# A vision tower on one core: norms summed by accumulators, and a patch product split into float32r parts

## The reference, cut to what matters

```python
h = concat([cls, patches @ W_tok.T + b]) + pos           # 32 x 37 x 256
n = layernorm(h)                                         # then gamma, beta
z, c = sigmoid(n @ Wg.T + bg), n @ Wc.T + bc
hs = scan over tokens: s = (1 - z) * s + z * c           # along t
h = h + n + hs
g = gelu(layernorm(h) @ ternary(W_fc).T)                 # 1024 wide
h = h + (layernorm(g) * ln_w + ln_b) @ ternary(W_proj).T
h = h + attention(layernorm(h))                          # rope, causal, 37 x 37 per image
q = clip(round(layernorm(h) / scale), -127, 127)
h = h + (q * scale) @ (ternary_weight - 1).T + bias
# ternary(W) = sign(W) * min(round(|W| / gamma), 1), gamma = mean(|W|) + 1e-6
```

## Time and profile before

| | |
|---|---|
| median of 3 runs | 160.27 us (159.31 to 160.37) |
| the profiled execution | 159.69 us |
| its span in the trace | 157.9 us |
| mean granted TensorE clock | 0.978 |
| busy PE, DVE, ACT, POOL | 139.8, 126.4, 96.0, 87.2 us |

### The profile page before, as it was taken

One profiled execution on the slowest core, in us unless ns is written; L12 is line 12 of the kernel. 1 busy time (PEld: TensorE's weight loads), 2 busy tenths in 40 slices (PEclk: granted clock), 3 DMA queues, 4 the chain that ended last, 5 costly groups with the idle time before them and its releaser, 6 DMA issues.

```text
span 157.9 us, 3087 instructions
## 1 busy us (share of the span) xinstructions
PE 139.8 (89%) x874; PEld 111.3 (71%) x874; DVE 126.4 (80%) x404; ACT 96.0 (61%) x232; POOL 87.2 (55%) x159
## 2 busy tenths in 40 slices
PE   0599999999999996967996999789989989699993
PEld 0479898999889973545682757779878978596551
DVE  0031479989999998999996999699898979859893
ACT  3102288169264779999978785972476066368350
POOL 0000183455353657288995539989845786663530
PEclk9999999999999999999999999999999999869995
DMA  5999996000410000096595755797310000000243
GB/s 163 258 398 425 421 391 238 2 0 0 124 46 0 2 2 2 18 119 133 125 111 104 162 113 108 147 106 149 60 55 0 4 0 0 2 4 0 65 144 103
DMA packets 25621, 17.00 MB, mean 108 GB/s; under 512 B 20069, under 2 KB 23173, under 8 KB 25349
## 3 DMA queue, kind: packets, MB, share of 16 engines
q1 hardware_dynamic: 25605, 16.81, 40.3%
HBM read 9.70 MB, written 1.21 MB: 69 GB/s over the span
## 4 chain that ended last, share of the span: by engine, by line
DVE 26%; PE 22%; POOL 21%; issue 11%; ACT 8%; DMA 6%; SPq 4%; DVEq 0%; POOLq 0%; ACTq 0%
POOL small L1540 8%; DMA w_out_int<-w_out_in 6%; PE bank L661 5%; SPq L463 4%; POOL keys L1619 4%; POOL small L1535 4%; PE bank L758 3%; DVE stats L1093 3%; DVE gw L1414 3%; DVE gl L1106 2%; PE bank L832 2%; PE bank L792 2%; DVE rope L1460 2%; POOL small L1544 2%; POOL residual L1592 2%
## 5 line engine op out<-in xcount | busy, mean ns | idle before, releaser
L1540 POOL TENSOR_TENSOR small<-small,powers 128x1 f32<-128x1 f32 (+4 forms) x48 | 39.7, 826 | 6.0 <-DVE small L1403 2.8
L661 PE MATMUL bank<-w_tok,x_raw 128*128 128x256 f32 x108 | 27.7, 411 | 5.8 <-DMA w_tok<-w_tok_in 5.6
L661 PEld LDWEIGHTS bank<-w_tok,x_raw 128*128 128x128 f32 x108 | 21.5, 206 | 8.8 <-issue 5.6
L1535 POOL TENSOR_SCALAR small<-small 128x1 f32<-128x1 f32 x36 | 9.4, 260 | 24.9 <-DVE small L1101 23.2
L537 PE MATMUL bank<-pj,gt_hi 128*128 128x256 f16 x72 | 16.2, 273 | 0.7 <-issue 0.7
L537 PE MATMUL bank<-pj,gt_lo 128*128 128x256 f16 x72 | 16.2, 273 | 0.0
L932 ACT ACTIVATE n<-residual,small 128x256 f32<-128x256 f32 x18 | 10.7, 595 | 9.0 <-POOL small L1544 9.0
L537 PE MATMUL bank<-fc,n1t_hi 128*128 128x512 f16 x36 | 13.6, 379 | 0.6 <-ACT g L1002 0.3
L537 PE MATMUL bank<-fc,n1t_lo 128*128 128x512 f16 x36 | 13.6, 379 | 0.0
L1460 DVE SCALAR_TENSOR_TENSOR rope<-bank,packed,consts 128x324 f32<-128x324 f32 (+2 forms) x24 | 13.1, 608 | 0.3 <-POOL query L1613 0.2
L932 ACT ACTIVATE s<-end,small 108x256 f32<-108x256 f32 (+2 forms) x12 | 7.2, 596 | 9.4 <-POOL small L1544 6.2
(11 more groups left out here) (199 smaller groups left out, 411.7 us busy)
## 6 DMA issues: line engine op xcount, KB each, us to landing
x_raw<-x_in SPq DMA_DIRECT2D x9, 384.0 KB, 7.8
out_dram<-end SPq DMA_DIRECT2D x10, 108.0 KB
w_fc<-w_fc_in SPq DMA_DIRECT2D x1, 1024.0 KB, 10.0
w_pj<-w_pj_in SPq DMA_DIRECT2D x1, 1024.0 KB, 13.0
w_tok<-w_tok_in SPq DMA_DIRECT2D x2, 384.0 KB, 4.6
w_gate<-w_gate_in SPq DMA_DIRECT2D x1, 512.0 KB, 7.3
w_qk<-w_qk_in SPq DMA_DIRECT2D x1, 512.0 KB, 12.5
ln_w<-ln_w_in SPq DMA_DIRECT2D x1, 512.0 KB, 3.6
```

The costliest lines, as they stand in the source:

```text
L661: mm(out[:, 0:D], x_raw[:, i, k, :], w_tok[:, k, :], start=(k == 0), stop=False)
L1535: return nc.gpsimd.tensor_scalar(small[0:n, i, out:out + 1], small[0:n, i, value:value + 1], factor, add, ALU.mult, ALU.add)
L1540: return gt(small[0:n, i, r:r + width], small[0:n, i, ve:ve + width], powers[0:n, 0:width], ALU.pow)
```

## The change

**Patches.** Tiles 0 and 1 stay as they are (`PLAIN = 2`). For tiles 2 to 8, ACT copies the tile (128x768) into x_hi, rounded to float32r, and the DVE writes the rest x_lo over x_raw. w_tok is split once in the same way (128x1536 on either engine). `tok` then takes 18 float32r products instead of 6 float32 ones. x_hi has three slots, which lie over the memory of the scan's result, so that `scan:0` waits for the last `tok`, and `split:5` and later wait for the `tok` three tiles before.

**Norms 1 to 3.** BN_STATS and BN_AGGR go. The DVE instruction that makes the new residual (h1, proj, attend, c_row) leaves its row sum in an accumulator. ACT squares the centred tile with an accumulator (step `sq`) in place of the Identity, a small DVE instruction makes the mean, and POOL applies mean and scale by one tensor_scalar over 128x256 (L1619 of the changed kernel) in place of the shift. For norm 0 the statistics stay on the DVE, and the application goes from the DVE to POOL.

**Weights.** The ternary weights come from ACT: scale and round in place (`w_round`), then Sign (`w_sign`), both 128x2048 for each weight. The DVE's four instructions go.

**Narrow products.** The norm bias is made of 16 products of 2 columns (`w_ln_col`), a DVE sum and two float32 products of 128 columns that spread it. The class sums 0, 1 and 3 take one product each, from an accumulator.

```diff
@@ -33,6 +33,8 @@
...
+PLAIN = 2
+X_SLOTS = 3
@@ -125,59 +127,60 @@
...
-        c_h0:0 w_ones:0 w_pos:0 c_mean:0 c_var:0 w_small:0 stats0:0 mean0:0 stats0:1 stats0:2 c_norm:0 mean0:1
...
+        w_ones:0 w_pos:0 w_tok:0 stats0:0 mean0:0 split:2 w_gate:0 c_h0:0 split:3 stats0:1 c_mean:0 split:4 mean0:1
@@ -345,6 +355,8 @@
...
+    x_hi = m.at("x_hi", [X_SLOTS, KX, TILE], F32R, b_at + both)
+    assert X_SLOTS * KX * TILE * 4 <= both
@@ -573,15 +587,25 @@
...
                 pe.wait_ge(s["ln_b_hi_ready"], 1)
                 pe.wait_ge(s["ln_b_lo_ready"], 1)
-                split_product(out[:, 0:D], [
-                    (part[:, k:k + 1].to_broadcast([128, 128]), pj[:, k, :])
-                    for k in range(KH) for part in (ln_b_hi, ln_b_lo)
-                ]).then_inc(s["pe_ln_bias"], 1)
+                for b in range(KD):
+                    last = split_product(out[:, 2 * b:2 * b + 2], [
+                        (pj[:, k, b * 128:(b + 1) * 128], ln_b_both[:, k, :]) for k in range(KH)])
...
+            def w_ln_bias(_i):
+                out = claim(NARROW, ("ln_bias", 0))
...
+                for k in range(KD):
+                    last = mm(out[:, k * 128:(k + 1) * 128],
+                              derived[:, D_LN_COL + k:D_LN_COL + k + 1].to_broadcast([128, 128]), ident,
+                              start=True, stop=True)
@@ -590,11 +614,11 @@
...
-                    columns = range(C_SOURCE[n], C_SOURCE[n] + KD)
-                split_product(out[:, 0:1], [(ones[:, :], cls[:, c:c + 1]) for c in columns])\
+                    column = C_HSUM + n
+                mm(out[:, 0:1], ones[:, :], cls[:, column:column + 1], start=True, stop=True)\
@@ -654,11 +678,23 @@
...
-                    mm(out[:, 0:D], x_raw[:, i, k, :], w_tok[:, k, :], start=(k == 0), stop=False)
+                if i < PLAIN:
+                    pe.wait_ge(dma_x[i], 16)
+                    for k in range(KX):
+                        if i == 0 and k % (KX // 2) == 0:
+                            pe.wait_ge(s["dma_w_tok_b" if k else "dma_w_tok"], 16)
+                        mm(out[:, 0:D], x_raw[:, i, k, :], w_tok[:, k, :], start=(k == 0), stop=False)
+                else:
+                    if i == PLAIN:
+                        pe.wait_ge(s["wt_hi_ready"], 1)
+                        pe.wait_ge(s["wt_lo_ready"], 1)
+                    pe.wait_ge(s["x_hi_ready"], i - PLAIN + 1)
+                    pe.wait_ge(s["x_lo_ready"], i - PLAIN + 1)
+                    for k in range(KX):
+                        hi, lo = x_hi[:, i % X_SLOTS, k, :], x_lo[:, i, k, :]
+                        mm(out[:, 0:D], hi, wt_hi[:, k, :], start=(k == 0), stop=False)
+                        mm(out[:, 0:D], hi, wt_lo[:, k, :], start=False, stop=False)
+                        mm(out[:, 0:D], lo, wt_hi[:, k, :], start=False, stop=False)
@@ -890,6 +926,21 @@
...
+            def w_round(n):
+                _, w, _ = ternary[n]
+                act.wait_ge(s["cut_ready"], 2)
+                act.wait_ge(s["round_ready"], 2)
+                go(w[:, :, :], w[:, :, :], ACT.Identity, scale=derived[:, D_INV_GAMMA + n:D_INV_GAMMA + n + 1],
+                   bias=derived[:, D_ROUND:D_ROUND + 1]).then_inc(s["rounded_ready"], 1)
+            def w_sign(n):
+                out, w, ready = ternary[n]
+                act.wait_ge(s["rounded_ready"], n + 1)
+                go(out[:, :, :], w[:, :, :], ACT.Sign, bias=derived[:, D_ROUND + 1:D_ROUND + 2]).then_inc(s[ready], 1)
@@ -920,6 +971,17 @@
...
+            def w_tok_(_i):
+                act.wait_ge(s["dma_w_tok"], 16)
+                act.wait_ge(s["dma_w_tok_b"], 16)
+                go(wt_hi[:, :, :], w_tok[:, :, :], ACT.Copy).then_inc(s["wt_hi_ready"], 1)
+            def split(i):
+                act.wait_ge(dma_x[i], 16)
+                if i - PLAIN >= X_SLOTS:
+                    act.wait_ge(s["pe_tok"], i - X_SLOTS + 1)
+                go(x_hi[:, i % X_SLOTS, :, :], x_raw[:, i, :, :], ACT.Copy).then_inc(s["x_hi_ready"], 1)
@@ -937,29 +999,24 @@
...
+            def squares_of(norm):
+                def stage(i):
+                    h, ready, total, slot, free = summed[norm]
+                    n = end_rows(i) if norm == 3 else 128
+                    act.wait_ge(s[ready], i + 1)
+                    if i >= 2:
+                        act.wait_ge(s[free], i - 1)
+                    if i == 0 and norm == 2:
+                        act.wait_ge(s["pe_fold"], KD)
+                    if i == 0 and norm == 3:
+                        act.wait_ge(s["pe_gate"], 4 * CHUNKS)
+                    go(slot[0:n, i % 2, :], h[0:n, i, :], ACT.Square, bias=small[0:n, i, total:total + 1], scale=-float(D),
+                       accum_out=small[0:n, i, total + 1:total + 2]).then_inc(s[f"mv{norm}_ready"], 1)
+                return stage
@@ -1102,11 +1159,30 @@
...
+            def mean_of_sum(norm):
+                def stage(i):
+                    n = norm_rows(norm, i)
+                    dve.wait_ge(s[normed[norm][1]], i + 1)
+                    ts(col(i, MEANS[norm], 1, n), col(i, normed[norm][2], 1, n), 1.0 / D, None, ALU.mult)\
+                        .then_inc(s[f"mean{norm}_ready"], 1)
+                return stage
...
             def w_ones(_i):
                 nc.vector.memset(ones[:, :], 1.0).then_inc(s["ones_ready"], 1)
+                nc.vector.memset(derived[:, D_ROUND:D_ROUND + 1], ROUND).then_inc(s["round_ready"], 1)
+                nc.vector.memset(derived[:, D_ROUND + 1:D_ROUND + 2], -ROUND).then_inc(s["round_ready"], 1)
+            def w_tok_(_i):
+                dve.wait_ge(s["wt_hi_ready"], 1)
+                low_part(wt_lo[:, :, :], w_tok[:, :, :], wt_hi[:, :, :].bitcast(F32), s["wt_lo_ready"])
+            def split(i):
+                dve.wait_ge(s["x_hi_ready"], i - PLAIN + 1)
+                low_part(x_lo[:, i, :, :], x_raw[:, i, :, :], x_hi[:, i % X_SLOTS, :, :].bitcast(F32), s["x_lo_ready"])
@@ -1196,23 +1272,17 @@
...
-            def w_below(n):
-                out, w, _ = ternary[n]
-                dve.wait_ge(s["cut_ready"], 2)
-                ts(out[:, :, :], w[:, :, :], derived[:, D_NEG_CUT + n:D_NEG_CUT + n + 1], None, ALU.is_lt)\
-                    .then_inc(s["below_ready"], 1)
-            def w_ternary(n):
-                out, w, ready = ternary[n]
-                dve.wait_ge(s["below_ready"], n + 1)
-                stt(out=out[:, :, :], in0=w[:, :, :], scalar=derived[:, D_CUT + n:D_CUT + n + 1], in1=out[:, :, :],
-                    op0=ALU.is_gt, op1=ALU.subtract).then_inc(s[ready], 1)
+                ts(derived[:, D_GAMMA:D_GAMMA + 2], total, 1.0 / (HID * D), ABS_EPS, ALU.mult, ALU.add)\
+                    .then_inc(s["cut_ready"], 1)
@@ -1332,12 +1405,8 @@
...
             def n0_(i):
                 dve.wait_ge(s["r0_ready"], i + 1)
-                if i >= 2:
-                    dve.wait_ge(s["pe_t0"], i - 1)
                 shift(i, NB0, MV0, R0, "nb0_ready")
                 ts(col(i, NB0 + 1), col(i, R0), 1.0, None, ALU.add).then_inc(s["nb0_ready"], 1)
-                ts(n0[:, i % 2, :], h0[:, i, :], col(i, MV0), col(i, R0 + 1), ALU.subtract, ALU.mult)\
-                    .then_inc(s["n0_ready"], 1)
@@ -1376,6 +1445,8 @@
...
+                if n == 0:
+                    dve.wait_ge(s["pe_tok"], TILES)
                 if c > 0:
                     dve.wait_ge(s["hs_ready"], n - 1)
@@ -1385,7 +1456,8 @@
             def h1_(i):
                 dve.wait_ge(s["pe_hs"], i + 1)
                 dve.wait_ge(s["res0_ready"], i + 1)
-                tt(res[:, i, :], narrow(("hs", i)), res[:, i, :], ALU.add).then_inc(s["h1_ready"], 1)
+                stt(out=res[:, i, :], in0=narrow(("hs", i)), scalar=1.0, in1=res[:, i, :], op0=ALU.mult, op1=ALU.add,
+                    accum_out=col(i, MV1)).then_inc(s["h1_ready"], 1)
@@ -1539,10 +1614,10 @@
...
+            def applied(out, h, i, mv, r, n=128):
+                return nc.gpsimd.tensor_scalar(out, h[0:n, i, :], small[0:n, i, mv:mv + 1], small[0:n, i, r:r + 1],
+                                               ALU.subtract, ALU.mult)
@@ -1573,13 +1648,24 @@
...
+            def n0_(i):
+                pool.wait_ge(s["r0_ready"], i + 1)
+                if i >= 2:
+                    pool.wait_ge(s["pe_t0"], i - 1)
+                applied(n0[:, i % 2, :], h0, i, MV0, R0 + 1).then_inc(s["n0_ready"], 1)
             def h1_(i):
                 pool.wait_ge(s["mv1_ready"], i + 1)
-                scaled(i, VE1, MV1 + 1, 1.0, LN_EPS).then_inc(s["ve1_ready"], 1)
+                scaled(i, VE1, MV1 + 1, 1.0 / SQUARED, LN_EPS).then_inc(s["ve1_ready"], 1)
                 pool.wait_ge(s["ve1_ready"], i + 1)
                 power(i, VE1, R1).then_inc(s["r1_ready"], 1)
+            def n1_(i):
                 pool.wait_ge(s["r1_ready"], i + 1)
-                shift(i, NB1, MV1, R1, "nb1_ready")
+                if i >= 2:
+                    pool.wait_ge(s["pe_t1"], i - 1)
```

(2 more changed lines are left out.)

263 lines of the change are left out of this document (137 added, 126 removed).

## The result

The changed kernel takes **169.25 us**, median of four runs (167.54 to 171.16), against 160.32 of the kernel before in the same session: ratio 1.051, 95% interval 1.042 to 1.060. Two of the four runs are near 171 (the profiled one among them, 171.16 with a span of 169.4) and two near 167.6, and every ratio in this document is taken over the quicker runs of both kernels, while medians are over all runs. The forecast was 156.0. The sign is wrong, and the time lies outside the range.

The account below looks back on a forecast made before the run. No engine bounds the whole: PE decides from 20 to 60 us, the DVE leads the MLP, POOL beside it at its end. Front -1.7, MLP -0.8 and attention -1.2 from 159.69 gave 156.0 us, range 151.0 to 162.3.

Parts of the forecast that it names:

- Norms in the MLP: 60 to 110 us: DVE relief of 2.35 us against 1.6 for POOL's applications at 0.6 each; -0.8 us.
- The attention's term: 110 to 150 us: PE gains half of its 2.5 us idle time as the DVE loses 3.8; -1.2 us.
- The rival on POOL: MLP's end and attention: applications stretched to 1.1 us make POOL the bound; 162.3 us, chance 0.19.
- The hole at the start: PE before tile 2: waits for class token's sum, tile 2 at 15.9 to 17.0; 1.2 us lost.
- Patches: Tiles 2 to 8 on PE: 18 products in 2.08 us instead of 2.41; 2.3 us saved over seven tiles.
- Splits: Front: each tile costs the DVE 0.92 and ACT 0.8 us, w_tok some 1.8 and 1.5; nothing beyond the start.
- Front: Up to the first gelu: mean of PE's -2.1 us and ACT's -1.2; -1.7 us.
- Norm bias and class sums: Weight stages on PE: narrow products save 0.9 us on the norm bias and 0.1 on each class sum.
- ACT in the front: 20 to 60 us: ACT's busy time rises from 26.98 to 37.8 of 40 us.
- The rival, that no engine reaches such a share without loss: Front: ACT becomes the bound, its work taking 42 us at 90% busy; 159.9 us, chance 0.17.
- Norm rows on the DVE: MLP: 0.32 us less for each of some 15 norm rows, 4.8 us of DVE, of which 2.35 count.
- The rival that the MLP follows the DVE: 60 to 110 us: the DVE leads everywhere, so all 4.8 us count; 152.0 us, chance 0.22.

Follow-up runs that it names:

- e1: The kernel before with 14 extra POOL instructions of several forms in its idle time at the start; 158.75 us in one run.
- e3: The changed kernel with the class token's sum moved back to first place in the DVE's row; 167.05 us, ratio 1.047 to the kernel before.
- e5: e3 with the 39 POOL applications as a product of two tensors, the mean not subtracted; 154.41 us, ratio 0.964 to the kernel before.
- e15: e8 with the DVE's sum placed early and the spreading product and its DVE step moved behind the second h1; 161.66 us, ratio 1.011.
- e4: The changed kernel with all 39 norm applications on the DVE, the other engines' orders kept; 192.53 us, ratio 1.206 to the kernel before.
- e6: The kernel before with split patches and the ternary weights on ACT, norms as before, orders by hand; 171.48 us, ratio 1.061.
- e7: e6 with the narrow norm bias as well, orders by hand; 171.55 us, ratio 1.063 to the kernel before.
- e13: e4's instructions (applications on the DVE) in orders from a second, more robust search; 158.51 us, ratio 0.987 to the kernel before.
- e14: e7's instructions (norms as before) in orders from a second, more robust search; 155.76 us, ratio 0.978 to the kernel before.
- e8: The kernel before with the narrow norm bias alone; 162.61 us, ratio 1.008.

## Why the prediction was wrong, by its steps

**The step that failed** is, in "Norms in the MLP": "It has one, so I take 0.6, +0.22 each", with 0.38 to 0.728 as bounds and 1.1 as the end with stretch. The application takes 1.22 bare (e1) and 1.47 on the mean in norms 1 and 2, so the change is +1.09 each and not +0.22. The end of 1.1 was meant for applications stretched beside the DVE, and the price is above it without any. The reasoning behind it was that an instruction with one full input cannot cost more than one with two. e1 shows the reverse on POOL: 1.22 and 0.93 with one input and two or one operands by column, 0.61 with two inputs. The other bound, a shift of one column (0.378), says nothing of the 256 elements: e1 has 0.39 at the least for one column in the application's form and 1.22 for 256. I had no row of a wide tensor_scalar on POOL, and should have set a bound above the sum's 0.728, not only for stretch.

By the forecast's own formula 1.47 gives the MLP 15 x 1.09 x half - 2.35 = +5.8 in place of -0.8. Measured in e3: +2.2 (54.9 to 57.1), so less of the price showed there than the formula's half. The attention's term, -1.2, became +6.4 with the tail (43.3 to 49.7), which the forecast had at nothing: on POOL 12 applications of norm 3 take 14.8 us there in e3, where before 13 small shifts took 3.4. A part of the 6.4 is the clock, 0.90 on the mean there in e3 and 0.92 before. With the price taken back (e5) the same stages read -1.2 and -0.7 against before; the forecast had -0.8 and -1.2, and the front gave -4.0 for -1.7. So behind the front the sum held within 0.5 us a stage once its largest term had the price that it assumed (0.71 in e5, 0.6 in the forecast); that e5's 154.4 lies below 156.0 is the front's doing.

**The rival on POOL** had the mechanism and the place right, the end of the MLP (15.59 of 16.6 busy) and the attention, and its sign, applications above 1 us, came. The point from which it decides, about 1.0, no run tests: there are 0.71 (faster) and 1.4 (slower). It was given 0.19 and priced at 1.1, 162.3, which made the range end there. At the bare 1.22 it would already have passed. The rule that I quoted from the Trainium skill (GPSIMD Engine Reference, "Key points"), that elementwise work runs about twice as fast on VectorE, deserved more weight: by it and the 0.403 of the earlier trace rows an application would take some 0.8, an estimate, and that is above my bound of 0.728. The trace goes beyond it: 1.22 bare on POOL against 0.403 for the same tensor_scalar on the DVE, three times.

**The hole at the start**: forecast 15.9 to 17.0, near 16.4; measured 16.40, so the hole against 15.55 is 0.85, where the sum took 1.2. The wait that I named is there: the class token's sum is done on the DVE at 15.59, within the 15.1 to 16 of the forecast. Beside it stands one that I had not named: ACT's copy of tile 1 out of its bank, behind a split and the gate's high part, is done at 15.67, and it is the releaser that the trace gives. In e3, with `c_h0:0` in front, only that copy is left, and tile 2 starts at 15.59, near its place before; the class token's sum was worth 0.8. No term had the granted clock of 0.50 behind the hole in the profiled execution, some 3 us. Before, small products of PE filled the 0.87 us ahead of tile 2 almost wholly, and the clock was 1.00 there; after, PE had a pause of 1.68.

**Patches**: 18 products in 2.09 us (26.92 to 29.01), forecast 2.08. **Splits**: DVE 0.955 and 1.76, forecast 0.92 and 1.8; ACT 0.836, forecast 0.8. **Front**: forecast -1.7 with the hole in it; the first gelu of the changed kernel's trace is at 62.02, +2.3. With the hole repaired it is -1.5 (e3), close to the forecast by luck: without the 1.2 of the hole the forecast's way of reckoning gives some -2.3 (PE -3.3, ACT -1.2, for which it shows no working). With the POOL price gone as well it is -4.0 (e5). So the applications ahead of the first gelu, nine of norm 0, which I had called hidden in POOL's idle half, and two of norm 1, held it up by 2.5. That is a second term put at nothing.

**Norm bias and class sums**: the products cost what was forecast (0.55 for 0.54), but the term of 0.9 was not on the path. A stretch without idle time of PE is no proof that each microsecond taken from PE shortens it; with the DVE at 93% PE only waited instead (e15: 2.31 us of new waits, both for the DVE).

**ACT in the front**: 37.8 of 40 forecast, 37.61 in e3 and 39.60 in e5. The rival, that no engine reaches such a share without loss, is refuted by e5.

**Norm rows on the DVE**: 0.144 and an accumulator read of 0.083 for 0.413 and 0.171, so -0.357 each, forecast -0.32. The DVE was right to be unburdened, and it had the gain: 43.68 of 50 for 46.18, 2.5 us less, where the forecast had some 4. It went unused while POOL was late (e3), and part of it showed once POOL was not (e5).

**The rival that the MLP follows the DVE** can't be judged as a whole; e5, with POOL out of the way, gains 1.2 there and not 4.8, so the full count was too much.

## What to carry to other kernels

Where a change puts wide work on an engine that has only done narrow or different work in the trace, the nearest rows bound nothing from above: take the price as open, work out from which value on it decides (here about 1.0 us by the forecast's sum), and give that side its full chance. Then multiply: 39 instructions that were 0.7 us dearer in e3 than in e5 were 13 us of span, more than all other terms together. And a part that is moved between engines with a fixed row of work can only be judged with orders made for it; e4, e6 and e7 were 6 to 21% slower than before, and the instructions of e4 and e7 in other orders (e13, e14) were 1 to 2% faster.

## What the runs showed of the hardware

- POOL's tensor_scalar over 128x256 float32 takes 1.22 us with two operands by column, 1.08 and 1.15 with two constants, and 0.92 and 0.93 with one operand by column; its sum of two tensors of that size takes 0.61 (e1, DVE idle), and in e5 the product with a column spread over the tile 0.709 on the mean. A pair of such operations in place of the application would so save nothing: twice 0.61 is 1.22, and twice 0.709 is 1.42, for 1.22 and 1.47 (an estimate from these rows; no pair was run). Only a norm that needs a single one on POOL is cheaper.
- In the changed kernel the same application lasts up to 2.30 us, with a median of 1.23. The two longest, 2.27 from 94.72 and 2.30 from 98.01, ran beside the DVE's `gw` (1.29 from 94.76 and 1.28 from 97.93); that the one stretches the other is an inference from such pairs, and no run tests it. The powers of one column on POOL, whose stretch had worried me, take 0.646 on the mean, and took 0.858 before.
- The granted clock fell to 0.50 behind a pause of PE of 1.68 us (the changed kernel, from 17.5 us on), of 2.69 (e8), of 1.79 (e5, from 75.5), of 1.05 (e14, from 22.5) and of 1.09 (before, from 137). It stayed at 1.00 behind pauses of 0.92 (e3), 1.31 (e15), 1.55 and 1.96 (e3, before 120.5 and 84.0), and behind the same 1.09 in e8. So the length of the pause alone does not decide it, and these traces do not show what does.
- Reading an accumulator costs 0.083 us on the DVE and 0.199 on ACT, as an instruction of its own (in the changed kernel, 18 on each of the two engines in norms 1 and 2).
